# A new order of layer 2 on all engines, its scaled delta kept in PSUM, and slot rows of layer 3 loaded four tiles at a time

## The chip, the cores and the metric

The program runs on 1 core of one Trainium2 chip. The metric is the device time of one execution in microseconds (us), lower is better. Engines are named PE (TensorE matmul), PEld (TensorE weight load), DVE (VectorE), ACT (ScalarE), POOL (GpSimd) and SP (the engine that here only issues DMAs). L2222 is line 2222 of the kernel file before the change.

## The reference

Four layers, each an attention block and a feed-forward block, on x of shape (16, 128, 256), float32, all added to x behind a gate tanh(g). The change touches two of the blocks and nothing that is computed.

```python
# layer 2, attention: 16 heads of 16, keys and values from ctx
q, k, v = proj(x_norm, Wq, bq), proj(ctx, Wk, bk), proj(ctx, Wv, bv)
probs = softmax(clip(q @ k.T / 4, -50, 50))          # masked keys at -50
delta = rs * ((probs @ v) @ Wo.T + bo)
delta = (delta - delta.mean()) / sqrt(delta.var() + 1e-5) * ln_gamma + ln_beta
x = x + tanh(g_xattn[2]) * delta
# layer 2, feed-forward: weights rounded to -1, 0, 1, activations to 8 bits
h = silu(bitlinear(norm(x), w_gate)) * bitlinear(norm(x), w_up)   # 832 wide
x = x + tanh(g_ffn[2]) * bitlinear(h, w_down)
# layer 3, feed-forward: 64 experts of width 96, 6 of them for each token,
# at most 64 tokens per expert and sequence group, and a shared expert of width 192
gx = xp[buf_tok]; g, u = split(gx @ gate_up); eo = (silu(g) * u) @ down * buf_w
x = x + tanh(g_ffn[3]) * (scatter_add(eo) + shared(x))
```

## The kernel before, in words

There is no scheduler. Each layer writes out by hand one program for each engine, and semaphores join them; an engine runs its program strictly in order, so an instruction that waits holds all behind it.

**Layer 2** (`layer_2`). One loop of 19 steps i works on three of the 16 sequences (blocks of 128 tokens) at once: attention of block i, the add of the attention and the start of the feed-forward for y = i - 2, and the end of the feed-forward for f = i - 3. Up to i = 12 each step also produces the keys or the queries of a later pair of blocks ("paired" steps): PE projects (L2127 keys, L2144 queries), ACT adds the bias and rounds to bf16 (`act_bias`, `act_hi`), POOL takes the rest (`pool_rest`, L2603), ACT rounds it (`act_mid`), POOL takes what is left (`pool_lo`, L2607), SP stores the three parts to DRAM and loads them back as stacks for the scores. Even steps also norm a coming pair (`dve_norm_stats`, `pool_norm`).

The work of one step, by name. PE: `pe_scores` twice (half the heads each), `pe_turn_x` in odd steps, `pe_turn_hq` (L2228), `pe_weigh` twice (L2186, probabilities by values, all into one PSUM bank, `av_bank`), `pe_down` (L2235), `pe_values` (L2157), `pe_turn_xq` (L2211), `pe_up` (L2222, gate half and then up half, eight matmuls), `pe_project_out` (L2195, L2197, also into `av_bank`). DVE: `dve_ffn_gate` (L2404 to L2417: the gating, a maximum and the rounding of h), `dve_add_attention` (L2369 scales the delta from PSUM into SBUF, L2373 adds it to x), `dve_ffn_stats`, `dve_clip` twice (L2339), `dve_ffn_quantise` (L2385 to L2394), `dve_normalise` twice (L2347 to L2356), `dve_ffn_add` (L2422), and `dve_delta_stats` (L2361 to L2365) last in the step. ACT: `act_exp` twice, the steps of the production, `act_less_mean`, `act_keep_hq`, `act_values`, `act_keep_xq`, `act_tanh` (L2533). POOL: `pool_delta_root` (L2612, the power -1/2 that L2373 waits for) first in the step, then rest and lo.

In PE's order of before, `pe_project_out(i - 1)` stands last in step i, right behind `pe_up`; the second `pe_weigh` of a block waits until L2369 has read the bank.

**Layer 3, experts** (`l3_experts`). 32 tiles, each two experts by 64 slots. Before them and after them the shared expert runs over 8 blocks. A tile: PE turns its rows (L3366), multiplies by gate and up weights (L3377), turns the hidden part (L3385), multiplies by the down weights (L3392); DVE finds in the rows the tile's own weights and targets (`dve_own`, L3496 to L3502) and gates; ACT scales into `ye_t` (L3569); POOL scatters that to DRAM (L3614). Stages of four tiles are in work at once. SP, one queue, first issues weights of tiles 0 to 9 (576 KB a tile), waits until the slot rows are complete in DRAM, issues the rows of tiles 0 to 5 (140 KB a tile), weights 10 to 19, and then in turn rows n + 6 and weights n + 20 as buffers come free. `dve_own(n)` also waits for the scatter of tile n - 6 (`y_out`), since its target list lies in one of six buffers; `act_store(n)` has the same wait for its `ye_t`.

## Time and profile before

| | |
|---|---|
| median of 3 runs | 2377.92 us (2376.22 to 2381.36) |
| the profiled execution | 2375.99 us, of which 2374.7 us are the span from first to last instruction |
| busy share of the span | PE 83%, DVE 65%, ACT 38%, POOL 23% |
| mean granted PE clock | 0.904 of full speed |
| loop of layer 2 | about 1297 to 1610 us |
| tiles of the experts of layer 3 | about 2237 to 2326 us |

A row of the timeline is one instruction or several of one line merged: start, length, engine, line, operation, count, and in brackets the idle time of the engine before it with what ended that. A row of the waits sums idle time by the pair of waiting line and releasing line. PEclk is the clock granted to TensorE, as a share of its full speed (1.00 is 2.4 GHz, 0.50 is 1.2 GHz); a mixed value is a stretch with both. A DMA share of 1 means that all 16 DMA engines were busy.

### The profile page before, as it was taken

Reading aid. Unit: us, or ns where it says so; the run is one execution under the profiler, and the core shown is the slowest. Engines: PE = TensorE matmul, PEld = TensorE weight load, DVE = VectorE, ACT = ScalarE, POOL = GpSimd, SP = SyncE. Lnnn points to the kernel's source line nnn. Section 1 sums busy time; section 2 is a strip of 40 time slices with the busy share of each in tenths; the row PEclk is TensorE's granted clock in tenths of the full one; section 3 lists DMA queues with packets and bytes.
Section 4 is the critical chain, followed back from the end, with each engine's and each line's share of the span. In section 5 each row is a group of like instructions: output and inputs, shape, how many; then the busy total and the mean of one; then the engine's idle time right before and its main releaser. Section 6 shows DMA issues by size and latency. Waiting matters only on the chain.

```text
span 2374.7 us, 35012 instructions
## 1 busy us (share of the span) xinstructions
PE 1970.2 (83%) x12412; PEld 1270.1 (53%) x12412; DVE 1547.9 (65%) x3614; ACT 907.0 (38%) x2073; POOL 552.8 (23%) x671
## 2 busy tenths in 40 slices
PE   6888889999994878888696677666799999987697
PEld 2444446555553767766523444434467666666344
DVE  7888844444438999999713877762456666655457
ACT  2666631111112655666413444321344443433242
POOL 2212110000002333332303444211013332333231
PEclk7999999999996998999798887767899999998879
DMA  4442220000003333332201452208000000000966
GB/s 97 137 120 61 52 77 14 1 0 1 0 1 81 72 79 73 71 77 59 69 0 47 125 121 64 54 1 274 20 1 30 30 17 4 1 1 1 252 208 266
DMA packets 160348, 157.89 MB, mean 66 GB/s; under 512 B 84504, under 2 KB 139040, under 8 KB 156240
## 3 DMA queue, kind: packets, MB, share of 16 engines
q1 hardware_dynamic: 150864, 146.18, 23.1%
q0 software_dynamic: 6144, 8.82, 1.1%
q8 instruction: 100, 1.64, 0.3%
q10 hardware_dynamic: 3168, 0.66, 0.1%
q14 instruction: 72, 0.59, 0.1%
HBM read 103.14 MB, written 60.82 MB: 69 GB/s over the span
## 4 chain that ended last, share of the span: by engine, by line
PE 56%; DVE 28%; issue 7%; ACT 5%; DMA 2%; POOL 1%; SPq 0%; ACTq 0%; DVEq 0%; POOLq 0%
PE psum L984 10%; PE psum L1004 5%; PE psum L2886 4%; PE psum L2812 3%; PE psum L382 3%; DVE sbuf L535 2%; PE psum L1892 2%; DVE sbuf L1540 2%; PE psum L2879 2%; DVE sbuf L1547 2%; PE psum L2861 2%; PE psum L345 2%; PE psum L2222 1%; PE psum L2848 1%; PE psum L2235 1%
## 5 line engine op out<-in xcount | busy, mean ns | idle before, releaser
L984 PE MATMUL psum<-sbuf 128*128 128x512 f32 (+1 forms) x544 | 245.7, 594 | 0.0
L182 POOL TENSOR_TENSOR sbuf<-sbuf 128x1 f32<-128x1 f32 x128 | 78.0, 612 | 716.8 <-DVE sbuf L174 716.3
L535 DVE TENSOR_REDUCE sbuf<-psum 128x2 f32<-128x512 f32 x256 | 164.8, 684 | 32.4 <-PE psum L345 31.3
L3199 ACT ACTIVATE sbuf<-psum,sbuf 128x128 f32<-128x128 f32 x256 | 113.7, 454 | 188.3 <-DVE sbuf L3034 188.3
L1678 ACT ACTIVATE sbuf<-psum 128x512 f32<-128x512 f32 x256 | 139.8, 597 | 107.6 <-PE psum L1404 93.3
L1110 DVE SCALAR_TENSOR_TENSOR sbuf<-sbuf,psum 128x512 f32<-128x512 f32 (+1 forms) x68 | 46.8, 688 | 196.9 <-ACT sbuf L1173 196.9
L1173 ACT ACTIVATE sbuf<-psum 128x512 f32<-128x512 f32 (+1 forms) x68 | 40.6, 597 | 309.1 <-PE psum L984 309.1
L984 PEld LDWEIGHTS psum<-sbuf 128*128 128x128 f32 (+1 forms) x544 | 100.0, 187 | 105.6 <-issue 103.1
L682 ACT ACTIVATE sbuf<-psum 128x1024 f32<-128x1024 f32 x128 | 130.6, 1022 | 40.9 <-PE psum L367 33.9
L1004 PE MATMUL psum<-sbuf 128*128 128x256 f32 (+1 forms) x544 | 129.2, 380 | 0.7 <-DVE sbuf L1115 0.7
L2812 PE MATMUL psum<-sbuf 128*128 128x256 f32 x512 | 121.8, 393 | 3.4 <-DVE sbuf L2992 1.9
L345 PE MATMUL psum<-sbuf 112*128 112x256 bf16 x512 | 104.4, 289 | 23.1 <-DVE sbuf L535 17.4
L2886 PE MATMUL psum<-sbuf 128*128 128x256 f32 x512 | 121.4, 386 | 1.8 <-DVE sbuf L3048 1.8
L1004 PEld LDWEIGHTS psum<-sbuf 128*128 128x128 f32 (+1 forms) x544 | 102.5, 189 | 37.7 <-issue 24.0
L3271 POOL DMA_INDIRECT l_slot_inputs<-sbuf x96 | 95.4, 993 | 100.9 <-DVE sbuf L3105 67.6
L2812 PEld LDWEIGHTS psum<-sbuf 128*128 128x128 f32 x512 | 99.8, 198 | 25.3 <-issue 6.7
L2879 PE MATMUL psum<-sbuf 128*128 128x512 f32 x128 | 73.1, 654 | 43.5 <-ACT sbuf L3207 43.5
L2886 PEld LDWEIGHTS psum<-sbuf 128*128 128x128 f32 x512 | 95.8, 195 | 13.3 <-DVE sbuf L3048 1.9
L2992 DVE COPY sbuf<-psum 128x1024 f32<-128x1024 f32 x32 | 39.2, 1225 | 89.8 <-ACT sbuf L3170 89.6
L345 PEld LDWEIGHTS psum<-sbuf 112*128 112x128 bf16 x512 | 41.2, 100 | 102.1 <-DVE sbuf L535 64.1
L1547 DVE TENSOR_REDUCE sbuf<-psum 128x8 f32<-128x1024 f32 x64 | 78.0, 1219 | 14.1 <-PE psum L1395 14.1
L1429 PE MATMUL psum<-sbuf 128*16 128x128 f32 x2048 | 74.2, 289 | 13.7 <-DVE sbuf L1569 10.9
(395 smaller groups left out, 4475.5 us busy)
## 6 DMA issues: line engine op xcount, KB each, us to landing
l_pair_outputs<-sbuf SPq DMA_DIRECT2D x24, 512.0 KB, 7.1
sbuf<-in_l_gu_pairs SPq DMA_DIRECT2D x32, 384.0 KB, 7.4
sbuf<-l_pair_outputs SPq DMA_DIRECT2D x16, 768.0 KB, 15.5
sbuf<-l_q_parts SPq DMA_DIRECT2D x16, 384.0 KB
l_q_parts<-sbuf SPq DMA_DIRECT2D x64, 96.0 KB, 2.0
sbuf<-l_q_parts SPq DMA_DIRECT2D x32, 192.0 KB
l_k_parts<-sbuf SPq DMA_DIRECT2D x64, 96.0 KB, 2.0
sbuf<-l_k_parts SPq DMA_DIRECT2D x32, 192.0 KB
```

Source lines behind the costliest of these rows:

```text
L345: last = pe.matmul(score_bank[v % 2][:, j * T0:(j + 1) * T0], q3[0:STACK + 48, h, c * P:(c + 1) * P], k3[0:STACK + 48, h // 4, :], start=T ...
L535: dve.tensor_reduce(top3[:, 2 * hp:2 * hp + 2, c], score_bank[v % 2].rearrange("p (j t) -> p j t", j=2), AXX, ALU.max, negate=True).then_i ...
L682: act.activation(e_t[u % 12], shift_bank[u % 2], ACT.Exp).then_inc(*exped.up())
L984: last = pe.matmul(up_bank[v % 2][0:M, n * BANK:(n + 1) * BANK], wn[:, k, fs], xt_t[blk % 2][:, k, :], start=(k == 0), stop=(k == KD - 1))
L1004: last = pe.matmul(acc[:, i * D:(i + 1) * D], h_t[v % 3][0:M, i * P:(i + 1) * P], w.proj[0:M, f, :], start=(f == 0 and i % 2 == 0), stop=( ...
L1547: dve.tensor_reduce(top_t[b % 2][:, 8 * s:8 * s + 8], split_cols(adapter_bank, 8), AXX, ALU.max, negate=True).then_inc(*a_maxed.up())
L1678: act.activation(e_t[i % 4][:, h * BANK:(h + 1) * BANK], turn_bank[:, h * BANK:(h + 1) * BANK], ACT.Exp).then_inc(*exped.up())
L2812: last = pe.matmul(q_bank[:, j * N:(j + 1) * N], w.wq[:, k, (4 * g + j) * P:(4 * g + j + 1) * P], xt_t[pair % 2][:, k, :], start=(k == 0), ...
L2879: pe.matmul(av_bank, v_t[b % 3][:, g * P:(g + 1) * P], eT_t[u % 2], start=True, stop=True).then_inc(*valued.up())
L2886: last = pe.matmul(out_bank[:, 0:D], o_t[b % 2][:, h * P:(h + 1) * P], w.wo[:, h, :], start=(h == 0), stop=(h == H3 - 1))
L3199: last = act.activation(e_t[u % 3][:, j * P:(j + 1) * P], score_bank[:, j * P:(j + 1) * P], ACT.Exp, bias=mt[:, j:j + 1], scale=rq[:, lo + ...
L3271: pool.indirect_dma_start(out=route.x_slots[:, :], out_offset=bass.IndirectOffsetOnAxis(ap=route.slot[b][:, k:k + 1], axis=0), in_=xr_t[b ...
```

## The change

In layer 2 every engine's program gets another order. On PE the output projection of block y = i - 2 opens step i instead of closing step i - 1, the values come before the first `pe_weigh`, `pe_turn_xq` behind the second, and the first half of the scores of the next block is taken ahead of `pe_up`. On DVE `dve_delta_stats` moves from the end of the step to behind the gate. On ACT the first exp of the next block is done ahead of the tanh, and `act_keep_hq` and `act_values` come before `act_less_mean`. On POOL the root goes behind rest and lo. The scaled delta stays in PSUM: L2369 writes it in place over `av_bank`, L2373 reads it there, and the second `pe_weigh` therefore waits for L2373 (`x_mid`) instead of L2369. `pe_up` signals its gate half and its up half apart; the tanh waits for the first alone. There are four value buffers instead of three.

In layer 3 the rows are loaded four tiles to a DMA, 16 tiles' worth ahead of weights 10 to 19 (tiles 0 to 15 instead of 0 to 5), the later groups from the weight loop: tiles 16 to 19 ahead of weight 23, 20 to 23 ahead of weight 27, 24 to 27 ahead of weight 31, 28 to 31 last of all. `own_t` and `pair_t` exist once for each tile, and `dve_own` no longer waits for a scatter.

```diff
-    v_t = [mem.f32(H2 * 32) for _ in range(3)]
+    v_t = [mem.f32(H2 * 32) for _ in range(4)]
...
         elif b:
-            pe.wait_ge(*y_read.at(b))
+            pe.wait_ge(*x_mid.at(b))
...
-        last.then_inc(*upped.up())
+            last.then_inc(*upped.up())
...
     pe_program:
+        pe_scores(0)
         for i in range(NB + 3):
-            f, y = i - 3, i - 2
-            if i < NB:
-                pe_scores(2 * i)
-            if made_in(i) < 2 * NPAIR:
-                if i % 2 == 0:
-                    pe_queries(i // 2 + 1)
-                else:
-                    pe_keys(i // 2 + 2)
+            f, y, paired = i - 3, i - 2, made_in(i) < 2 * NPAIR
+            if 0 <= y < NB:
+                pe_project_out(y)
+            if paired and i % 2 == 0:
+                pe_queries(i // 2 + 1)
+            if paired and i % 2 == 1:
+                pe_keys(i // 2 + 2)
             if i < NB:
                 pe_scores(2 * i + 1)
...
             if f >= 0:
                 pe_turn_hq(f)
+            if i + 2 < NB:
+                pe_values(i + 2)
             if 1 <= i <= NB:
                 pe_weigh(2 * i - 1)
             if f >= 0:
                 pe_down(f)
-            if i + 2 < NB:
-                pe_values(i + 2)
-            if 0 <= y < NB:
-                pe_turn_xq(y)
             if i < NB:
                 pe_weigh(2 * i)
             if 0 <= y < NB:
+                pe_turn_xq(y)
+            if i + 1 < NB:
+                pe_scores(2 * i + 2)
+            if 0 <= y < NB:
                 pe_up(y)
-            if 1 <= i <= NB:
-                pe_project_out(i - 1)
...
-        d, s = y_t[b % 2][:, 0:D], y_t[b % 2][:, D:D + 16]
-        dve.scalar_tensor_tensor(d, av_bank[:, 0:D], s[:, 6:7], w.gamma, ALU.subtract, ALU.mult).then_inc(*y_read.up())
+        d, s = av_bank[:, 0:D], y_t[b % 2]
+        dve.scalar_tensor_tensor(d, d, s[:, 6:7], w.gamma, ALU.subtract, ALU.mult).then_inc(*y_scaled.up())
...
     dve_program:
             if f >= 0:
                 dve_ffn_gate(f)
             if 0 <= y < NB:
+                dve_delta_stats(y)
+            if i < NB:
+                dve_clip(2 * i)
+            if 0 <= y < NB:
                 dve_add_attention(y)
                 dve_ffn_stats(y)
-            if i < NB:
-                dve_clip(2 * i)
+            if 1 <= i <= NB:
+                dve_normalise(2 * i - 1)
+            if 0 <= y < NB:
+                dve_ffn_quantise(y)
             if i % 2 == 0 and i // 2 + 2 < NPAIR:
                 dve_norm_stats(i // 2 + 2)
-            if 0 <= y < NB:
-                dve_ffn_quantise(y)
-            if 1 <= i <= NB:
-                dve_normalise(2 * i - 1)
             if f >= 0:
                 dve_ffn_add(f)
...
-            if 1 <= i <= NB:
-                dve_delta_stats(i - 1)
...
     act_program:
+        act_exp(0)
...
-            if 0 <= y < NB:
-                act_less_mean(y)
             if f >= 0:
                 act_keep_hq(f)
             if i + 2 < NB:
                 act_values(i + 2)
             if 0 <= y < NB:
+                act_less_mean(y)
                 act_keep_xq(y)
+            if i + 1 < NB:
+                act_exp(2 * i + 2)
+            if 0 <= y < NB:
                 act_tanh(y)
...
     pool_program:
-            if 0 <= y < NB:
-                pool_delta_root(y)
             if j < 2 * NPAIR:
                 pool_rest(j)
                 pool_lo(j)
+            if 0 <= y < NB:
+                pool_delta_root(y)
...
     layer 3:
-        dve.wait_ge(*x_in[n % 6].at(16 * (n // 6 + 1)))
-        if n >= 6:
-            dve.wait_ge(*y_out[n % 6].at(16 * (n // 6)))
+        dve.wait_ge(*x_in[n // 4 % 4].at(16 * (n // 16 + 1)))
...
+    def sp_load_rows(g):
+        if g >= 4:
+            sp.wait_ge(*turned.at(4 * (g - 4) + 4))
+            sp.wait_ge(*own_ready.at(4 * (g - 4) + 4))
+        dst = xe_all[g % 4].rearrange("p (t n) -> p t n", t=4)
+        sp.dma_start(dst, route.x_slots[4 * g * P:4 * (g + 1) * P].rearrange("(t p) n -> p t n", t=4)).then_inc(*x_in[g % 4].up(16))
...
-        for n in range(6):
-            sp_load_rows(n)
+        for g in range(4):
+            sp_load_rows(g)
         for n in range(10, NW3):
             sp_load_weights(n)
-        for n in range(NP):
-            if n + 6 < NP:
-                sp_load_rows(n + 6)
-            if n + NW3 < NP:
-                sp_load_weights(n + NW3)
+        for n in range(NP - NW3):
+            if n in (3, 7, 11):
+                sp_load_rows(n // 4 + 4)
+            sp_load_weights(n + NW3)
+        sp_load_rows(7)
```

## Rows read from the trace of the kernel before

**Rows 1.** Timeline of VectorE, layer 2: start us, us, engine, line, operation
```profile
1392.02 1.02 DVE L2404 SCALAR_TENSOR_TENSOR sbuf<-sbuf,psum 128x832 f32<-128x832 f32 x1
...
1499.52 1.02 DVE L2404 SCALAR_TENSOR_TENSOR sbuf<-sbuf,psum 128x832 f32<-128x832 f32 x1
...
1600.65 1.02 DVE L2404 SCALAR_TENSOR_TENSOR sbuf<-sbuf,psum 128x832 f32<-128x832 f32 x1 [4.58 <-ACT sbuf L2533]
```

**Rows 2.** Waits of VectorE from 1392 to 1500: us in total, times, longest
```profile
DVE sbuf L2361 <- PE psum L2197: 11.5, 6, 2.3
...
DVE sbuf L2347 <- PE psum L2186: 8.0, 6, 2.3
```

**Rows 3.** Timeline of all engines in one loop step of layer 2
```profile
1435.38 0.42 DVE L170 BATCH_NORM_STATS2 sbuf<-sbuf 128x6 f32<-128x256 f32 x1
...
1436.86 0.41 DVE L2385 TENSOR_REDUCE sbuf<-sbuf 128x1 f32<-128x256 f32 x1
...
1438.34 0.44 DVE L2347 STREAM_TRANSPOSE sbuf<-psum 128x256 f32<-128x256 f32 x1
...
1439.61 0.44 DVE L2422 SCALAR_TENSOR_TENSOR sbuf<-psum,sbuf 128x256 f32<-128x256 f32 x1
...
1439.98 0.68 DVE L2339 TENSOR_SCALAR sbuf<-sbuf 128x1024 f32<-128x1024 f32 x1
...
1440.97 1.58 PE L2222 MATMUL psum<-sbuf 128*128 128x416 bf16 x8
...
1442.48 0.69 PE L2195 MATMUL psum<-sbuf 1*128 1x256 f32 x2
...
1444.27 0.43 DVE L2361 BATCH_NORM_STATS2 sbuf<-psum 128x6 f32<-128x256 f32 x1 [1.93 <-PE psum L2197]
...
1444.52 1.95 PE L2127 MATMUL psum<-sbuf 128*128 128x256 f32 x8
...
1445.05 1.02 DVE L2404 SCALAR_TENSOR_TENSOR sbuf<-sbuf,psum 128x832 f32<-128x832 f32 x1
...
1449.61 0.47 DVE L2369 SCALAR_TENSOR_TENSOR sbuf<-psum,sbuf 128x256 f32<-128x256 f32 x1
...
1450.18 1.15 POOL L2607 TENSOR_TENSOR sbuf<-sbuf 128x512 bf16<-128x512 f32 x1 [0.94 <-ACT sbuf L2503]
```

**Rows 4.** Groups by line and shape, 1319 to 1611: count, busy us, mean ns
```profile
L2373 DVE SCALAR_TENSOR_TENSOR sbuf<-sbuf 128x256 f32<-128x256 f32 x16 | 16.5, 1033 | 2.3 <-POOL sbuf L2612 0.3
...
L2612 POOL TENSOR_TENSOR sbuf<-sbuf 128x1 f32<-128x1 f32 x16 | 8.9, 553 | 92.6 <-DVE sbuf L2365 92.6
```

**Rows 5.** Timeline of TensorE before the loop of layer 2
```profile
1272.17 3.78 PE L2144 MATMUL psum<-sbuf 128*128 128x256 f32 x8 [0.69 <-ACT sbuf L2493]
```

**Rows 6.** Windows in layer 3: busy us of each engine, PEclk, DMA share, GB/s
```profile
2230.00:2246.00 16.00, 15.17 (x92) 7.89 (x90) 9.95 (x45) 5.69 (x21) 1.58 (x2) 1.00 1.01 283
...
2246.00:2254.00 8.00, 0.18 (x3) 0.09 (x2) 0.45 (x3) 0.47 (x1) 1.33 (x2) 0.67 1.05 306
...
2254.00:2286.00 32.00, 32.00 (x137) 13.81 (x137) 12.62 (x67) 9.69 (x27) 7.77 (x8) 0.50 0.91 266
...
2286.00:2320.00 34.00, 33.39 (x253) 16.77 (x251) 21.61 (x111) 16.77 (x51) 15.63 (x17) 0.99 0.45 142
```

**Rows 7.** The chain that ended last, in order of time: start, us, what
```profile
2238.82 15.05 DMA sbuf<-l_slot_inputs
```

**Rows 8.** Line 3366, the turning matmuls of the expert loop
```profile
L3366 PE MATMUL psum<-sbuf x64: 272/328/477, 2237.1 to 2318.7; 128*128 128x128 f32 x64
```

**Rows 9.** DMA issues from 2190 to 2345: KB each, median us to landing
```profile
sbuf<-in_l_gu_pairs SPq DMA_DIRECT2D x32, 384.0 KB, 7.4
...
sbuf<-l_slot_inputs SPq DMA_DIRECT2D x32, 140.0 KB
```

**Rows 10.** Waits of VectorE from 2254 to 2330
```profile
DVE sbuf L3496 <- DMA l_pair_outputs<-sbuf: 4.5, 5, 1.9
```

**Rows 11.** Line 3614, the scatters of finished tiles
```profile
DMA to landing us min/median/max: 2.4/2.8/7.2
```

More of the change, by code:

```diff
@@ L2072, in layer_2 @@
     stack = {n: [mem.bf16(H2 * S) for _ in range(2)] for n in "kq"}
-    v_t = [mem.f32(H2 * 32) for _ in range(3)]
+    v_t = [mem.f32(H2 * 32) for _ in range(4)]
     attn_t = [mem.f32(2 * P) for _ in range(2)]
-    y_t = [mem.f32(D + 16) for _ in range(2)]
+    y_t = [mem.f32(16) for _ in range(2)]
     ones, minus_round, row = mem.f32(P), mem.f32(1), mem.f32(D, 1)
@@ L2358, in dve_delta_stats @@
     def dve_delta_stats(b):
-        s, chain = y_t[b % 2][:, D:D + 16], m.chain
+        s, chain = y_t[b % 2], m.chain
         dve.wait_ge(*projected.at(b + 1))
@@ L2609, in pool_delta_root @@
     def pool_delta_root(b):
[L2610 removed]
+        s = y_t[b % 2][:, 8:9]
         pool.wait_ge(*y_var.at(b + 1))
@@ L3332, in l3_experts @@
     sh_t = [mem.f32(SI3) for _ in range(2)]
-    xe_t = [mem.f32(DX) for _ in range(6)]
     xeT_t = [mem.f32(D) for _ in range(2)]
@@ L3337, in l3_experts @@
     ye_t = [mem.f32(D) for _ in range(6)]
-    eq_t, prod_t, own_t = mem.f32(K3), split_cols(mem.f32(2 * K3), 2), [mem.f32(2) for _ in range(6)]
-    pair_t = [mem.f32(1).bitcast(U32) for _ in range(6)]
+    xe_all = [mem.f32(4 * DX) for _ in range(4)]
+    xe_t = [a[:, i * DX:(i + 1) * DX] for a in xe_all for i in range(4)]
+    eq_t, prod_t, own_t = mem.f32(K3), split_cols(mem.f32(2 * K3), 2), [mem.f32(2) for _ in range(NP)]
+    pair_t = [mem.f32(1).bitcast(U32) for _ in range(NP)]
     late = Arena(m.sbuf, B_AT, m.l3_attention_end)
@@ L3344, in l3_experts @@
     w_in = [m.mark(f"expert_weights_loaded_{i}") for i in range(NW3 // 2)]
-    x_in = [m.mark(f"rows_loaded_{i}") for i in range(6)]
+    x_in = [m.mark(f"rows_loaded_{i}") for i in range(4)]
     y_out = [m.mark(f"pairs_scattered_{i}") for i in range(6)]
@@ L3501, in dve_own @@
         dve.wait_ge(*m.chain.now())
-        dve.tensor_scalar(pair_t[n % 6], own[:, 1:2], float(NTOP3), None, ALU.add).then_inc(*own_ready.up())
+        dve.tensor_scalar(pair_t[n], own[:, 1:2], float(NTOP3), None, ALU.add).then_inc(*own_ready.up())
     def dve_combine(b):
```

37 lines of the change are left out of this document (15 added, 22 removed).

## The prediction

> **What bounds the kernel now.** I first read the page: PE is busy for 83% of the span, DVE for 65%, but these are averages over eight blocks of which the change touches two, some 400 of 2375 us. So I read the two stages one at a time, each with the timeline, the waits, and windows.
>
> In layer 2 the thing to see is the step length. `dve_ffn_gate` opens each step, so its first instruction is the step's clock: between the 4th and the 10th of its 16 runs lie six steps of 17.92 us, between the 10th and the last six of 16.86 us [rows 1]. Inside a step DVE stands idle 3.3 us: 11.5 us in six steps for the output projection (L2361) and 8.0 us for the weighing (L2347) [rows 2]. PE in turn waits for the rounded h and for its copy. Neither engine is full; they hand one chain back and forth. Hence order matters, and less work doesn't help unless it lies on that chain.
>
> In layer 3 there are 32 tiles. The turning of the last starts at 2318.7, that of the first at 2237.1 [rows 8]. Three stretches follow each other [rows 6]. Up to 2246 the clock is 1.00, with DMA full at 283 GB/s. From 2246 to 2254 nothing runs: tile 6's rows, issued at 2238.82 behind ten tiles of weights, land 15.05 us later [rows 7]. From 2254 to 2286 the clock is 0.50, and 137 matmuls (15 a tile) are 9 tiles, 3.5 us each; after that, 253 matmuls in 34 us are 2.0 us a tile. The stall costs 7.8 us itself and 9 x 1.5 = 14 us by the slow clock behind it.
>
> **Layer 2, step by step.** I lay measured pieces end to end in the new order, from one start of `pe_up` to the next, in a paired step. The pieces are start-to-start distances in rows 3, so hand-offs are in them.
> - `pe_up` to `pe_project_out`: 1440.97 to 1442.48, 1.5 us. Projection: its reader L2361 starts 1.8 us behind it, at 1444.27, and keys or queries, with no scores between them any more, can follow a little sooner: 1.6.
> - Keys or queries, bias, hi, rest, mid, lo: 1444.52 to the end of L2607 at 1451.33, 6.8 us. The root now stands behind this on POOL: 0.55 [rows 4].
> - L2373, which now reads PSUM, taken at 0.48 (below), the statistics 0.83 (two of them take 1.48, 1435.38 to 1436.86, and an unshared one a little more than half), hand-offs 0.15. Sum so far 11.9 us.
> - The weighing waits for x_mid and delivers 0.3 us after the statistics are done; one normalise is 1.27 (1438.34 to 1439.61), the quantise 1.48 (1436.86 to 1438.34): 14.95.
> - Even steps: two norm statistics 1.48 and the add 0.37 (1439.61 to 1439.98), then `pe_up`: 16.85. Odd steps: turn, copy and hand-offs, 1.0: 15.95.
>
> The mean is 16.4. PE's clock will be low in some of the short matmuls behind a wait, as it is now; I add 0.25: 16.65, against 17.92, a saving of 1.3 us. This holds for steps 3 to 12 at least, nine of them up to the 10th gate: 9 x 1.3 = 11.5 us. So the DVE wait for the projection goes, but what is late next is the root: DVE has finished gate, delta statistics and clip (4.56 + 0.78 + 0.60) some 2 us before `pool_lo` and the root are through, and waits for POOL where it never did.
>
> In the unpaired steps that cover is gone and DVE's own list decides: gate 4.56 (1445.05 to 1449.61), delta statistics 0.78 (1444.27 to 1445.05), two clips 1.2, the two delta instructions 1.0, statistics 0.83, two normalises 2.54, quantise 1.48, add 0.37: 12.8. With 1.6 us of waits for root, weighing and tanh it is 14.4. The last six steps are one paired and five of these: (16.65 + 5 x 14.4) / 6 = 14.8 against 16.86, 6 x 2.06 = 12.4 us. Layer 2 saves 11.5 + 12.4, say 24 us.
>
> Edits inside that sum. The tanh starts after the gate half of `pe_up`: 4 of 8 matmuls earlier, 0.75 us, but the exp now ahead of it on ACT eats about as much; it is in the 1.6. The delta in PSUM: L2373 takes 1.03 us on average with both inputs in SBUF [rows 4], L2422, the same operation and shape with one input in PSUM, 0.44 [rows 3]. I take 0.48; bounds 0.44 and 1.03, that is 0 to 0.6 us a step, so up to 9 us less gain. Writing PSUM from DVE appears in no row; nearest is L2369's 0.47 into SBUF, taken unchanged, up to 1.0 as the far bound (8 us). The extra memset of a value buffer, 0.5 us, lies before the wait of DVE for the weight sums, on no path. The second weighing waits for L2373 instead of L2369, 0.5 us later plus the root; behind it on PE are down, the first weighing and turn_xq, counted. Stacks: scores of the next block are taken a few us earlier in a step, while their DMAs are issued a whole step before; cover some 9 us.
>
> L2422 shows no price for a PSUM source. The Trainium skill (VectorE: DVE Perf Modes, the TRN2 errata) gives VectorE 120 fixed cycles for a PSUM source and 58 for SBUF, which speaks against this edit; by it, an estimate, L2373 would be 0.065 us dearer, 1.0 us over 16 steps. By the row it is nothing.
>
> **Layer 3, step by step.** Tiles 6 to 15 are there early, so the stall at tile 6 goes (7.8 us), and with it the fall of the clock (14 us): 21.8 us on paper. But DMA is full from 2230 on, and bytes do not go away. A tile's weights are 384 KB [rows 9] and 192 KB, its rows 140 KB. SP is one queue and the rows of tiles 20 to 23 are issued behind rows 0 to 19 and weights 10 to 26: 24 x 0.143 + 17 x 0.590 = 13.5 MB, plus 16 scatters of 0.13 MB, 15.6 MB in all. At 283 GB/s [rows 6] from 2226 that is 55 us, 2281. At 2.0 us a tile PE wants them at 2237 + 40 = 2277: a stall of 4 us. Then 0.57 MB of rows, four weights and scatters, 3.4 MB, 12 us: tiles 24 to 27 at 2293. The idle stretch at 2246 took the clock from 1.00 to 0.50 within it (0.67 mean over 8 us, [rows 6]), so I take it that 4 us do that too. Then tiles 20 to 28 go at 3.5 us as nine tiles did, the clock comes back at about 2313, and the last turn is at 2313 + 2 = 2315, against 2318.7: a gain of 4 us. Bounds: the clock never comes back, 2281 + 11 x 3.5 = 2319.5, nothing gained; the clock holds, tile 24 at 2293, the last at 2307, 12 us; DMA at 306 GB/s [rows 6], 16 us.
>
> The stall falls between dense stretches. The Trainium skill (TensorE: Matmul & The Clock Gate, HAM oscillation) tells of a loop in which each wait for DMA returns the array to its low clock; by that rule layer 3 gains the 4 us and not the 12.
>
> `dve_own`'s waits for scatters, 4.5 us in five times [rows 10], go. `act_store` keeps such a wait, but six tiles, 12 us, after the scatter it waits for; landings take at most 7.2 [rows 11]. SP's later loads wait for tiles long turned.
>
> **The sum.** -24 - 4 = -28 us on the profiled execution's 2375.99: 2348. The median of the runs shown lies 1.9 us above the profiled one, so 2350.
>
> **The rivals.**
> - *The clock holds.* The new order spreads PE's waits into more and shorter ones (I lay 1.1, 2.4 and 1.5 us in a paired step), and layer 2 keeps 1.00 through the matmuls behind them. At half the clock eight matmuls of the same size take 3.78 us [rows 5] instead of 1.9, so these run twice as fast; with 2 us of them slow in four steps of ten, an estimate, that is 0.8 us a step, 12 us in 15 steps. In layer 3 the stall is below what costs the clock: 12 instead of 4. 2350 - 20 = 2330. For it: the gap that cost the clock in layer 3 was 8 us long. Against: more pieces of work stand behind a wait.
> - *Half lost to the root.* Keys and queries stand on the chain now. At the low clock they take 3.78 us [rows 5], not 1.95 [rows 3], and the projection, in the same ratio less its fixed part, 2.9, not 1.6: 3.2 us a step. If that hits half of the ten paired steps, 16 us are gone, and 2 of layer 3: 2368. Against it: keys and projection run right behind `pe_up` at the high clock now [rows 3], and the new order keeps this neighbour.
> - *Slower.* The same place, all ten steps: 32 us lost in layer 2, 8 us above before, and layer 3 gains nothing: 2386. The mechanism decides from 28 / 3.2 = 9 of the ten steps on. For it only that the chain leaves no cover; the rest as above.
> - *Nothing.* The saved waits return elsewhere to the last microsecond: within 0.2%, which is 4.8 us and about what a measurement of this kernel can tell from no change.
>
> **How the numbers follow.** The forecast (its own range 2340 to 2360) has 0.45, the clock holds 0.28, half lost 0.15, slower 0.09, nothing 0.03. The range 2326 to 2372 takes in the first three and leaves out 0.15 or so. Faster 0.87, same 0.04, slower 0.09.
>
> **What would show it.** Layer 2: gate to gate 16 to 17.5 us, alternating, and 14 to 15 after the last paired step; L2373 near 0.5 us, and a new wait of DVE for POOL's root of about 2 us in paired steps, none in the others; the DVE wait for the projection near zero. A wait below 1 us there, or a step above 17.5, proves the chain wrong. Layer 3: no gap at 2246 less the shift; rows of tiles 20 or 24 awaited 3 to 5 us; the clock in the 30 us behind. If that gap is missing, the DMA sum is wrong, and the time falls to the low end. If L2361 or the weighing still waits 2 us a step, PE's list is longer than I laid it, and the gain halves.

## The result, and the profile after

The changed kernel takes 2354.89 us (median of four, 2344.89 to 2359.69) beside 2379.64 us for the kernel before: a ratio of 0.9886 (95% interval 0.9844 to 0.9929), 25 us faster on medians. The profiled execution is the fastest of the four, 2344.89 us with a span of 2343.5 us, and so 10 us below the median; the sums of this section are made on the spans of the two profiled executions, which differ by 31.2 us. Line numbers of the changed kernel are up to three higher: L2422, L2612, L3052 and L3366 of before are now L2423, L2614, L3054 and L3369.

**Layer 2.** The timeline of the changed kernel at the same three runs of the gate as [rows 1], the 4th, the 10th and the last:

```profile
1389.12 1.02 DVE L2404 SCALAR_TENSOR_TENSOR sbuf<-sbuf,psum 128x832 f32<-128x832 f32 x1 [0.80 <-ACT sbuf L2534]
...
1492.35 1.02 DVE L2404 SCALAR_TENSOR_TENSOR sbuf<-sbuf,psum 128x832 f32<-128x832 f32 x1 [0.80 <-ACT sbuf L2534]
...
1581.20 1.02 DVE L2404 SCALAR_TENSOR_TENSOR sbuf<-sbuf,psum 128x832 f32<-128x832 f32 x1 [3.49 <-ACT sbuf L2534]
```

From the 4th to the 10th are 103.2 us, 17.2 a step (17.92 before), from the 10th to the last 88.9 us, 14.8 a step (16.86). The last add of layer 2 comes at 1590.80, 19.4 us earlier than before. The waits of VectorE between 1392 and 1500, which answer to [rows 2]:

```profile
DVE sbuf L2373 <- POOL sbuf L2614: 15.7, 6, 5.1
...
DVE sbuf L2404 <- ACT sbuf L2534: 4.8, 6, 1.0
...
DVE sbuf L2347 <- PE psum L2186: 0.4, 1, 0.4
```

The waits for the projection are gone and the one for the weighing has shrunk to 0.4 us. In their place stand a wait for the root, 2.6 us a step, and one for the tanh, 0.8 us a step. The groups by line and shape answer to [rows 4]:

```profile
L2369 DVE SCALAR_TENSOR_TENSOR psum<-psum,sbuf 128x256 f32<-128x256 f32 x16 | 7.7, 484 | 0.0
...
L2373 DVE SCALAR_TENSOR_TENSOR sbuf<-psum,sbuf 128x256 f32<-128x256 f32 x16 | 7.7, 483 | 27.5 <-POOL sbuf L2614 27.1
```

The write of the delta into PSUM takes 0.484 us, and L2373, which reads it there, 0.483 us, as against 1.033 on average before.

**Layer 3, experts.** Windows over the stage (busy us of PE, PEld, DVE, ACT and POOL, then PEclk, DMA share, GB/s), which answer to [rows 6]:

```profile
2219.00:2235.00 16.00, 15.17 (x87) 8.18 (x87) 9.17 (x42) 5.65 (x21) 0.97 (x1) 1.00 1.06 334
...
2235.00:2251.00 16.00, 16.00 (x122) 8.09 (x122) 10.71 (x57) 8.02 (x26) 7.79 (x8) 1.00 1.04 336
...
2251.00:2267.00 16.00, 16.00 (x122) 8.07 (x121) 10.72 (x57) 8.02 (x26) 7.79 (x8) 1.00 1.05 334
...
2267.00:2275.00 8.00, 6.59 (x53) 3.31 (x49) 4.64 (x24) 3.39 (x11) 3.80 (x4) 1.00 1.06 328
```

The line of the turning matmuls answers to [rows 8]:

```profile
L3369 PE MATMUL psum<-sbuf x64: 272/273/332, 2227.5 to 2288.0; 128*128 128x128 f32 x64
```

The first turn is at 2227.5, the last at 2288.0: 60.5 us, where it was 81.6. There is no idle stretch at tile 6, the clock stays at 1.00, and at a full DMA share 328 to 336 GB/s are moved, where [rows 6] had 283 to 306. Only at the turn of tile 24, near 2273, is there a gap, of 1.4 us. The trace puts it down to VectorE's L3469, for which this turn doesn't wait; the tile's rows were issued at 2259.09, and their late arrival is my reading, not shown.

**The account** of the 31.2 us: layer 2 gives 19.4, the experts 21.1, what follows them 0.5. Between layer 2 and the experts, where nothing was changed, 9.8 us are lost. The line that adds the attention of layer 3, once for each of 16 blocks, shows most of it; in the kernel before (first row), in the changed one (second), and in the experiment with rows asked for sooner (third), whose code is the same up to there:

```profile
L3052 DVE SCALAR_TENSOR_TENSOR sbuf<-psum,sbuf x16: 476/478/480, 1740.9 to 2197.6; 128x256 f32<-128x256 f32 x16
```

```profile
L3054 DVE SCALAR_TENSOR_TENSOR sbuf<-psum,sbuf x16: 476/477/482, 1721.5 to 2187.4; 128x256 f32<-128x256 f32 x16
```

```profile
L3054 DVE SCALAR_TENSOR_TENSOR sbuf<-psum,sbuf x16: 476/477/479, 1722.3 to 2177.7; 128x256 f32<-128x256 f32 x16
```

First to last: 456.7, 465.9 and 455.4 us. The same code took anything from 455 to 466 us in the profiles of this study, and the changed kernel itself took 457.2 in a second one. So these 9 us are no price of the change that every execution pays; they lie in the spread of single executions.

### The profile page after: what moved, and what is told of

It is laid out like the page before. It is cut to its first block, busy times and chain, and to the rows that moved or that the text cites. A ratio compares the mean times of both kernels' runs of the same rounds, so it can differ in the third digit from the quotient of the medians.

```text
span 2343.5 us, 34927 instructions
## 1 busy us (share of the span) xinstructions
PE 1949.3 (83%) x12382; PEld 1261.0 (54%) x12412; DVE 1538.9 (66%) x3616; ACT 905.9 (39%) x2073; POOL 553.2 (24%) x671
## 4 chain that ended last, share of the span: by engine, by line
PE 56%; DVE 27%; issue 7%; ACT 5%; POOL 2%; DMA 1%; SPq 0%; ACTq 0%; another core or an unknown queue 0%; DVEq 0%; POOLq 0%
PE psum L984 10%; PE psum L1004 5%; PE psum L2888 4%; PE psum L2814 4%; PE psum L382 3%; DVE sbuf L535 3%; PE psum L1892 2%; DVE sbuf L1540 2%; PE psum L2881 2%; PE psum L2863 2%; DVE sbuf L1547 2%; PE psum L345 2%; PE psum L2850 1%; PE psum L2222 1%; PE psum L367 1%
## 5 line engine op out<-in xcount | busy, mean ns | idle before, releaser
L345 PE MATMUL psum<-sbuf 112*128 112x256 bf16 x512 | 105.1, 290 | 21.9 <-DVE sbuf L535 17.3
```

The source lines that it names most:

```text
L345: last = pe.matmul(score_bank[v % 2][:, j * T0:(j + 1) * T0], q3[0:STACK + 48, h, c * P:(c + 1) * P], k3[0:STACK + 48, h // 4, :], start=T ...
```

## The experiments

All were run beside the kernel before on the same chip; a ratio is to that. There are four such sets, in which the kernel before took 2379.64 us (changed), 2377.54 (the two parts and the two places of the root), 2367.90 (the next four rows) and 2371.27 (the last four), so medians are compared within a set and ratios across. Of each kernel the table shows the median, and from its profile the two step lengths of layer 2 (4th to 10th gate, 10th to last) and the expert stage (first to last turn).

| kernel | median us | ratio (95% interval) | steps us | experts us |
|---|---|---|---|---|
| before | | | 17.9, 16.9 | 81.6 |
| changed | 2354.89 | 0.9886 (0.9844 to 0.9929) | 17.2, 14.8 | 60.5 |
| layer 2 part alone | 2363.71 | 0.9939 (0.9918 to 0.9960) | 17.0, 14.6 | 84.2 |
| layer 3 part alone | 2366.36 | 0.9946 (0.9924 to 0.9967) | 18.2, 16.3 | 65.9 |
| root between | 2334.57 | 0.9812 (0.9783 to 0.9840) | 15.5, 14.4 | 60.2 |
| root first | 2324.90 | 0.9786 (0.9757 to 0.9815) | 15.3, 14.5 | 60.1 |
| rows one by one | 2354.84 | 0.9921 (0.9891 to 0.9951) | 17.3, 14.9 | 79.7 |
| two groups late | 2341.71 | 0.9884 (0.9853 to 0.9914) | 17.3, 14.8 | 67.7 |
| delta in SBUF | 2342.39 | 0.9886 (0.9860 to 0.9913) | 17.1, 14.3 | 65.9 |
| one signal | 2350.35 | 0.9923 (0.9898 to 0.9948) | 17.1, 15.3 | 78.9 |
| changed, again | 2338.36 | 0.9853 (0.9832 to 0.9874) | 17.1, 14.4 | 78.3 |
| rows sooner | 2333.29 | 0.9832 (0.9812 to 0.9851) | 16.9, 15.0 | 59.1 |
| root first, rows sooner | 2315.55 | 0.9761 (0.9743 to 0.9779) | 15.3, 14.5 | 59.1 |
| the same, delta in SBUF | 2310.62 | 0.9742 (0.9723 to 0.9761) | 15.3, 14.2 | 59.1 |

The layer 2 of the changed kernel stands unedited in six rows (changed, layer 2 part alone, one by one, two late, again, sooner): its steps are 16.9 to 17.3 and 14.4 to 15.0 us. That is the noise against which a step is read. The layer 3 of the changed kernel stands unedited in seven rows, and its stage is anything from 60.1 to 78.9 us; the section on the slot rows comes back to that. A ratio therefore can't tell 5 us of layer 2 from the luck of layer 3.

### The two parts alone

The layer 2 part alone has layer 3 as before; the layer 3 part alone has layer 2 as before.

> The layer 2 part alone; layer 3's slot rows are loaded as in the kernel before. The theory (the two parts are independent): layer 2 keeps its new step times (f3 to f9 17.2 us a step, f9 to f15 14.8), its last x_done comes 19 us earlier, and the expert stage is the old one with its stall near tile 6 and the low clock behind it; about 19 us (15 to 20) faster than before, 0.992 of it. Rival 1 (layer 2's order costs the attention of layer 3 some 10 us through its clock, which is where the trace of the changed kernel lost them): about 10 us faster, and layer 3's block times drift against those of before as they did in the changed kernel. Rival 2 (that loss was the variation of one execution): no such drift here.

> The layer 3 part alone; layer 2 as in the kernel before. The theory (the stall at tile 6 was late rows, and its removal also keeps the clock): the expert stage runs 20 us shorter, with the granted clock at 1.00 throughout and no wait above 2 us; 18 to 21 us faster than before. Rival (the prediction's reading: the DMA rate of 283 GB/s sets the stage, and the changed kernel's 335 GB/s was luck of that execution): a stall of 4 us near tile 20 and a low clock behind it, 4 us faster. A third: the two parts do not add up, since their sum of 39 us is more than the 25 us by which the medians differ; then one of them gives less than its stage showed.

They give 13.8 and 11.2 us on medians, together 25.0, as much as the whole change: the parts add up, within intervals of some 5 us each. Neither hit its number. In the profile of the layer 2 part layer 2 is 21 us shorter, but the expert stage of before, stall and all, takes 84.2 us, not 81.6, and layer 3's attention 463 us; the drift is therefore there without being tied to a part (the layer 3 part alone shows 462). In the layer 3 part the stage shrank by 15.7 us, and it has waits for rows after all, 1.4 us at tile 20 and 2.6 at tile 24, as its waits of TensorE show (L3367 is its turning line):

```profile
PE psum L3367 <- DMA sbuf<-l_slot_inputs: 4.0, 2, 2.6
```

### The place of the root

```diff
             if j < 2 * NPAIR:
                 pool_rest(j)
-                pool_lo(j)
             if 0 <= y < NB:
                 pool_delta_root(y)
+            if j < 2 * NPAIR:
+                pool_lo(j)
```

That is the root between the two subtractions; in the other kernel it stands ahead of both, as before the change.

> The changed kernel with GpSimd's root of the variance put between its subtractions 'rest' and 'lo' of the paired steps, not behind both. The theory (the root comes late because two subtractions stand ahead of it): VectorE's wait for the root falls from 2.6 us a paired step to about 1.2, TensorE's wait for the scores' clip by the same, and ten paired steps are 1 us shorter each: 7 to 12 us faster than the changed kernel. Rival (the second subtraction then comes later, the 'lo' rows for the keys' turn are late, and TensorE waits there instead): the wait for the root falls and the step stays at 17.2 us.

> The changed kernel with GpSimd's root ahead of both subtractions, the place it had in the kernel before. The theory: VectorE's wait for the root falls to some 0.6 us, but GpSimd now stands at the root until VectorE has the variance, with both subtractions queued behind it; the gain is at most that of the root between them, 0 to 10 us faster than the changed kernel. Rival (the subtractions are on no path that matters): 2 us a paired step, 20 us faster. Other rival (they are, and their lateness costs more than the root's): slower than the changed kernel by 5 us or more.

The root first is faster than forecast: 0.9786, beside 0.9886 and (measured again) 0.9853 for the changed kernel, is 16 to 24 us. The root between gains 10 to 18 us by the same two ratios, and 7 to 12 were forecast. The paired step falls from 17.2 to 15.5 and 15.3 us, more than the 1 us forecast for the root between. The gates of the kernel with the root first:

```profile
1382.26 1.02 DVE L2404 SCALAR_TENSOR_TENSOR sbuf<-sbuf,psum 128x832 f32<-128x832 f32 x1 [0.81 <-ACT sbuf L2534]
...
1474.12 1.02 DVE L2404 SCALAR_TENSOR_TENSOR sbuf<-sbuf,psum 128x832 f32<-128x832 f32 x1 [1.75 <-ACT sbuf L2534]
...
1561.11 1.02 DVE L2404 SCALAR_TENSOR_TENSOR sbuf<-sbuf,psum 128x832 f32<-128x832 f32 x1 [3.49 <-ACT sbuf L2534]
```

Its waits from 1392 to 1500, of VectorE, of GpSimd and of TensorE, and under them those of VectorE with the root between:

```profile
DVE sbuf L2404 <- ACT sbuf L2534: 6.1, 7, 1.8
...
DVE sbuf L2347 <- PE psum L2186: 1.9, 3, 0.9
```

```profile
POOL sbuf L2614 <- DVE sbuf L2365: 42.3, 7, 8.4
```

```profile
PE psum L2235 <- ACT sbuf L2542: 7.6, 6, 1.5
...
PE psum L2186 <- DVE sbuf L2373: 1.8, 3, 0.6
```

```profile
DVE sbuf L2404 <- ACT sbuf L2534: 5.4, 7, 1.3
...
DVE sbuf L2373 <- POOL sbuf L2614: 5.1, 3, 2.8
```

With the root first no wait for it is left. GpSimd stands 42.3 us at the root until the variance is there, with both subtractions queued behind it. That lateness is not free: ScalarE, which rounds what the first subtraction leaves, comes later to the copy of h (L2542), and TensorE now waits 7.6 us for that. But its wait for L2373 before the weighing fell from 12.3 us in six times to 1.8 in three, and the balance is 1.9 us a step (1.6 in the pair of the last set, 16.9 to 15.3). So the rival was nearly right: the lateness of the subtractions costs less than that of the root, whose 0.55 us of work had been waiting behind 2.3 us of them. The root between keeps a third of the waits (5.1 us in three steps). The clean price is that of the last set, on one chip, rows sooner against rows sooner with the root first: 2333.29 (2329.88 to 2334.80) to 2315.55 (2314.87 to 2317.05), 17.7 us, and in their profiles 19 us from the first gate to the last add.

### The delta in PSUM

```diff
-        d, s = av_bank[:, 0:D], y_t[b % 2]
+        d, s = y_t[b % 2][:, 0:D], y_t[b % 2][:, D:D + 16]
-            pe.wait_ge(*x_mid.at(b))
+            pe.wait_ge(*y_scaled.at(b))
```

> The changed kernel with the scaled delta put back into SBUF, so that TensorE's weigh waits for the scaling alone and not for the addition to x behind the root. In the changed kernel TensorE waits for that addition 2.05 us a paired step. Theory (the PSUM delta ties TensorE to the root): that wait goes, values and weigh run 2.6 us sooner in a paired step, but VectorE still waits for the root itself, so the step shortens by 0.5 to 1.5 us only: 5 to 15 us faster than the changed kernel. Rival (VectorE is the bound of the step, its wait for the root stays, and the write to SBUF costs as much as that to PSUM): within 0.2% of the changed kernel.

> As the one beside it, and the scaled delta in SBUF, so that TensorE's weigh waits only for the scaling. With the delta in SBUF alone the last six steps of layer 2 took 14.25 us against 14.8, and the paired ones 17.07 against 17.2. Theory (with the root early, TensorE's wait for the addition to x is 0.3 us a step, and the PSUM delta still holds the bank through it): 0.3 to 0.5 us less in each of 16 steps, 4 to 8 us faster than the kernel beside it. Rival (with the root first the addition follows at once, and the bank comes free as soon either way): the same within 0.2%.

On the changed kernel it is the rival's case as far as can be told: its ratio of 0.9886 is that of the changed kernel (0.9886, and 0.9853 when run again), and the paired step is within the noise; its last six steps, 14.25 us, lie 0.15 under the lowest of the six rows. With the root first it is 4.9 us faster (2309.05 to 2313.44 against 2314.87 to 2317.05), but not by the mechanism expected: the first gate comes 1.6 us earlier in the profile, where nothing differs, and the last add of layer 2 only 0.3 us, so that layer 2 itself is no shorter; 4.2 us arise between that add and the first block of layer 3, where the granted clock is 0.73 and not 0.65 in the first 22 us. Why it is, stays open; that the clock there depends on how layer 2 ends is my guess.

The price of L2373 is clear, and it hangs on GpSimd as much as on the source that the prediction reasoned from. Its line in four kernels: before (SBUF), delta in SBUF on the changed kernel, root first (PSUM), and root first with the delta in SBUF:

```profile
L2373 DVE SCALAR_TENSOR_TENSOR sbuf<-sbuf x16: 483/1201/1409, 1324.4 to 1590.7; 128x256 f32<-128x256 f32 x16
```

```profile
L2373 DVE SCALAR_TENSOR_TENSOR sbuf<-sbuf x16: 483/485/485, 1331.9 to 1572.6; 128x256 f32<-128x256 f32 x16
```

```profile
L2373 DVE SCALAR_TENSOR_TENSOR sbuf<-psum,sbuf x16: 483/483/484, 1328.7 to 1553.6; 128x256 f32<-128x256 f32 x16
```

```profile
L2373 DVE SCALAR_TENSOR_TENSOR sbuf<-sbuf x16: 483/1284/1298, 1324.5 to 1550.8; 128x256 f32<-128x256 f32 x16
```

With both inputs in SBUF it takes 0.485 us when GpSimd waits beside it and a median of 1.28 when GpSimd subtracts; with one input in PSUM 0.483 in either case. The timelines of the last kernel and of the one with the root first show the neighbour, a subtraction of 1.15 us:

```profile
1448.71 1.15 POOL L2605 TENSOR_TENSOR sbuf<-sbuf 128x512 f32<-128x512 f32 x1
...
1448.86 1.28 DVE L2373 SCALAR_TENSOR_TENSOR sbuf<-sbuf 128x256 f32<-128x256 f32 x1
```

```profile
1449.52 1.15 POOL L2605 TENSOR_TENSOR sbuf<-sbuf 128x512 f32<-128x512 f32 x1
...
1449.68 0.48 DVE L2373 SCALAR_TENSOR_TENSOR sbuf<-psum,sbuf 128x256 f32<-128x256 f32 x1
```

The Trainium skill (GPSIMD Engine Reference, Specifications) says that VectorE and GpSimd share their SBUF interfaces and that a VectorE instruction with two SBUF inputs contends; these rows agree. The estimate of 65 ns more for a PSUM source, which the prediction worked out from the Trainium skill (VectorE: DVE Perf Modes, the TRN2 errata), is not borne out: 483 ns with one input in PSUM stand beside 485 with both in SBUF.

### One signal for both halves of the matmul

```diff
-        act.wait_ge(*upped.at(2 * f + 1))
+        act.wait_ge(*upped.at(2 * f + 2))
```

> The changed kernel, but the tanh waits for both halves of pe_up, as before, and not for the gate's half alone. Theory: the tanh starts one half of pe_up later (0.7 to 0.9 us of matmuls), and VectorE already waits 0.8 us a step for the tanh, so each of the sixteen steps is 0.5 to 0.9 us longer: 8 to 14 us slower than the changed kernel. Rival (VectorE comes to the gate later than that because of its wait for the root, and in the paired steps nothing changes): 2 to 5 us slower, from the last six steps alone.

The paired steps are as long as before (17.1 us), but not as they were. From 1392 to 1500 VectorE waits 8.0 us in six times for the tanh instead of 4.8, and for the root, 15.7 us in the changed kernel, not at all. The time went into VectorE's own instructions. L2418, the last instruction of `dve_ffn_gate`, in the changed kernel (first) and in this one:

```profile
L2418 DVE TENSOR_SCALAR sbuf<-sbuf x16: 653/654/655, 1341.3 to 1585.2; 128x832 f32<-128x832 f32 x16
```

```profile
L2418 DVE TENSOR_SCALAR sbuf<-sbuf x16: 653/1127/1607, 1342.3 to 1587.9; 128x832 f32<-128x832 f32 x16
```

In each of the six paired steps it takes 1.60 us and starts together with the first subtraction, and the clips (L2339) take 1.06 us on average instead of 0.76; one of the two runs beside the second subtraction. So the wait for the root was slack of VectorE, and the later start and the slower instructions used it up. The last six steps take 15.3 us, 0.3 above the noise. That is the rival's size, 2 to 5 us. The whole kernel is at 0.9923, but its profile also has a long expert stage, so that the ratio doesn't price the signal.

### The slot rows

Rows one by one: the same order and buffers, but a DMA for each tile.

```diff
-        sp.dma_start(dst, route.x_slots[4 * g * P:4 * (g + 1) * P].rearrange("(t p) n -> p t n", t=4)).then_inc(*x_in[g % 4].up(16))
+        for n in range(4 * g, 4 * g + 4):
+            sp.dma_start(xe_t[n % 16], route.x_slots[n * P:(n + 1) * P]).then_inc(*x_in[g % 4].up(16))
```

Two groups late: tiles 8 to 15 are asked for behind weights 10 to 19.

```diff
-        for g in range(4):
+        for g in range(2):
             sp_load_rows(g)
         for n in range(10, NW3):
             sp_load_weights(n)
+        for g in range(2, 4):
+            sp_load_rows(g)
```

> The changed kernel with the slot rows in the same order and the same 16 tiles of buffer, but loaded by one DMA for each tile of 140 KB, not one for four tiles of 560 KB. It separates the two things that the layer 3 part does. Theory A (the rows come in time because they are asked for ahead of the weights of tiles 10 to 19, and the form of the DMA is nothing): no stall in the expert loop, the granted clock stays at 1.00, last turn 60 us after the first, the same time as the changed kernel within 0.2%. Theory B (the DMA of four tiles is what raises the rate from the 280 GB/s of before to the 335 GB/s of after at the same full share): 280 to 300 GB/s in the first 24 us of the loop, so rows or weights come late near tile 16 to 20, a stall of 3 us or more there, a lower clock behind it, and 8 to 20 us slower than the changed kernel.

> The changed kernel with groups 2 and 3 of the slot rows (tiles 8 to 15) asked for behind the weights of tiles 10 to 19, and groups 0 and 1 ahead of them. Theory (what counts is what stands ahead of the rows in the queue): the weights of ten tiles are 5.9 MB, 17.6 us at 335 GB/s, and come behind 1.15 MB of rows; the rows of tile 8 land about 22 us behind the loop's start of loading and tile 8 is turned 16 us after the first; a stall of 5 to 9 us at tile 8, the granted clock falls to 0.50 behind it, and the stage takes 75 to 82 us, not 60.5; 13 to 20 us slower than the changed kernel. Rival (the stall alone, the clock holds): 6 us slower. Rival 2 (at 335 GB/s the rows come in time): no change.

One by one, theory B held for the rate. Its windows, and below them the waits of TensorE for rows:

```profile
2221.00:2237.00 16.00, 15.17 (x108) 7.96 (x108) 10.50 (x53) 6.56 (x21) 3.04 (x4) 1.00 1.00 279
...
2237.00:2253.00 16.00, 16.00 (x122) 8.09 (x124) 10.68 (x56) 8.02 (x25) 7.80 (x9) 1.00 1.04 327
...
2253.00:2258.00 5.00, 0.56 (x4) 0.10 (x4) 0.70 (x3) 0.50 (x2) 1.80 (x2) 0.89 1.06 332
```

```profile
PE psum L3369 <- DMA sbuf<-l_slot_inputs: 7.7, 3, 4.5
```

While the first 16 tiles of rows are under way, 279 GB/s are moved at a share of 1.00; in the next window, with few rows in it, 327. The rows come 7.7 us late in three times, PE is idle near 2255, and the stage takes 79.7 us. In the window at the same place, from 4 us ahead of the first turn, ten of the eleven profiles with DMAs of 560 KB show 315 to 338 GB/s, and one, that of one signal, 294. The Trainium skill (DMA: Bandwidth & Descriptors, Bandwidth) advises to batch DMAs, and its table, of single DMAs issued from GpSimd, has the rate rise with the size; these kernels agree in direction. Two things stay open. SP needed 8.8 us to issue the 16 DMAs where it needs 2.2 for four, and whether that or the size lowers the rate was not tried apart. And the 79.7 us are no price of the form by themselves, since the stage of the unedited kernel can be nearly as long, as the next profile shows. The late groups, however, came in time (theory wrong, rival 2 right for tile 8): only 0.3 us is lost there, and the stage's length of 67.7 us is due to a wait of 2.3 us at tile 24 and the low clock behind it.

That sends one back to the changed kernel, which was run again beside a kernel that asks for its last groups sooner:

```diff
-            if n in (3, 7, 11):
-                sp_load_rows(n // 4 + 4)
+            if n in (1, 5, 8, 10):
+                sp_load_rows({1: 4, 5: 5, 8: 6, 10: 7}[n])
             sp_load_weights(n + NW3)
-        sp_load_rows(7)
```

> The changed kernel itself, unedited, as the base for the three kernels beside it and to see whether its expert stage of 60.5 us is its usual one. Theory (the layer 3 part has little to spare: a group of rows lands late by a few us in some executions, near tile 16 or 24, and the clock falls behind it): the median is 0.988 to 0.991 of before, and this profile shows an expert stage from 60 to 80 us with waits for slot rows in it. Rival (the stage is always 60.5 us, and the executions differ elsewhere): 60 to 61 us here too.

> The changed kernel with the last four groups of slot rows asked for sooner among the weights: ahead of the weights of tiles 21, 25, 28 and 30, not of 23, 27, 31 and after the last. The buffers that they need are turned by then, so no wait is added. Theory (the late groups stand behind 1.7 MB of weights that are wanted later than they are): no wait for slot rows, the granted clock stays at 1.00, the expert stage takes 60 us, and the median is 4 to 12 us below the changed kernel's on the same chip, with less spread. Rival (the DMA engines are full until the last rows land, so that the total of bytes sets the wait and not its order): a wait of 2 to 5 us stays, now for weights, and the time is the same within 0.2%.

The unedited kernel in this second profile, by three windows, the waits of TensorE, and the chain that ended last (start, us, what):

```profile
2205.00:2221.00 16.00, 15.17 (x91) 8.12 (x89) 9.56 (x43) 5.66 (x20) 0.97 (x1) 1.00 1.06 338
...
2237.00:2253.00 16.00, 12.87 (x97) 6.36 (x95) 8.72 (x45) 6.72 (x20) 7.77 (x8) 0.97 1.05 323
...
2257.00:2283.00 26.00, 26.00 (x113) 11.40 (x113) 9.78 (x52) 8.62 (x23) 6.81 (x7) 0.50 0.43 127
```

```profile
PE psum L3369 <- DMA sbuf<-l_slot_inputs: 3.7, 1, 3.7
```

```profile
2236.72 16.77 DMA sbuf<-l_slot_inputs
```

The rows of tiles 20 to 23, issued at 2236.72, land 16.77 us later; PE waits 3.7 us, the clock falls to 0.50 for the next ten tiles, and the stage takes 78.3 us, 18 more than in the first profile of the very same program. With the rows sooner that group is issued at 2232.53, 15.4 us behind the first turn and not 23.8, and nothing waits for a slot row. Its issues on SP, windows, and turning line:

```profile
2232.53 1.57 SPq L3635 DMA_DIRECT2D sbuf<-l_slot_inputs  x1
```

```profile
2209.00:2225.00 16.00, 15.17 (x90) 8.31 (x90) 9.41 (x42) 5.65 (x20) 0.97 (x1) 1.00 1.06 344
...
2225.00:2241.00 16.00, 16.00 (x125) 8.07 (x122) 10.70 (x57) 7.98 (x24) 7.78 (x8) 1.00 1.05 334
...
2241.00:2257.00 16.00, 16.00 (x126) 8.07 (x120) 10.71 (x57) 7.97 (x24) 7.77 (x8) 1.00 1.05 344
...
2257.00:2263.00 6.00, 6.00 (x49) 3.02 (x45) 4.13 (x22) 2.99 (x9) 2.74 (x3) 1.00 1.07 324
```

```profile
L3369 PE MATMUL psum<-sbuf x64: 272/273/329, 2217.1 to 2276.2; 128*128 128x128 f32 x64
```

The DMA share is as full and the rate as high: order, not bytes.

Seven profiles of this study have the unedited layer 3. Of each the table shows how long before the first turn SP issues the first rows, the waits for rows at their tiles (with the gap at tile 24 that the trace of the changed kernel and that of the root first name otherwise), how long the clock is at 0.50 from there on, and the stage, all in us.

| kernel | first rows ahead | waits | low clock | experts |
|---|---|---|---|---|
| root first | 13.7 | 0.6 at tile 24 | none | 60.1 |
| root between | 13.5 | 1.1 at 24 | none | 60.2 |
| changed | 13.2 | 1.4 at 24 | none | 60.5 |
| delta in SBUF | 12.6 | 0.6 at 20, 3.1 at 24 | 7 | 65.9 |
| changed, again | 11.3 | 3.7 at 20 | 37 | 78.3 |
| one signal | 11.1 | 2.1 at 16 | 41 | 78.9 |
| layer 3 part alone | 11.0 | 1.4 at 20, 2.6 at 24 | 7 | 65.9 |

Where the rows are issued 13.2 us ahead or more, the stage is 60 us; where less, there is a wait with the low clock behind it. SP may issue them only when the slot rows are complete in DRAM, for which it waits 13.4 us in the changed kernel and 15.8 in its second profile. That is an order seen in seven profiles and was not set by an experiment. With the rows sooner the stage is 59.1 us in all three profiles, at 13.0, 12.2 and 11.8 us ahead.

The five runs with the rows sooner lie between 2329.88 and 2334.80, those of the unedited kernel between 2333.13 and 2348.56. The medians differ by 5.1 us, which the intervals don't separate; the upper half of the range is not seen again in five runs.

> The root of the variance ahead of both subtractions on GpSimd and the slot rows asked for sooner, both in one kernel. Theory (two stages, nothing shared): layer 2 as with the root first alone (15.3 us a paired step, last x_done at 1570 us), the expert stage 60 us, 2315 to 2325 us on a chip where the kernel before takes 2372, that is 0.976 to 0.980 of it. Rival (the shorter stage 2 is paid for by later clock falls in layer 3): no better than 0.981.

As the theory had it: 0.9761, five runs within 2.2 us of each other, 23 us (1.0%) under the changed kernel on that chip. With the delta in SBUF as well it is 0.9742, the fastest of all.

## Why the prediction was right, and where it was not

The forecast of 2350 us (faster) stands beside 2354.89, inside its own range. The sums of its two stages were off, in opposite directions.

- **The last six steps, 14.8 us.** Measured 14.8. In the five unpaired ones VectorE's own work and hand-offs are 12.0 us a step, not 12.8, and its waits 2.5 (12.3 in five, 8.5 of them for the tanh), not 1.6. The account had the right parts, and the errors of two of them cancel; that is luck.
- **The paired step, 16.65 us against 17.92.** Measured 17.2, and from the loop's start to the 10th gate 7 us were gained, not 11.5; that is nearly all of the difference between 24 and 19.4 us in layer 2. Five of the six steps up to there take 16.6 to 17.0 us, within 0.35 of the laid 16.65, and VectorE waits 2.1 us a step for the root in them (10.6 in five), as forecast. The sixth takes 19.15, with a wait of 5.1. The term mis-sized is therefore the 0.25 us a step laid for PE's low clock: the mean lies 0.56 above 16.65, and 0.42 of that is the sixth step alone. In it the rival *half lost to the root* is to be seen at work: in the timeline of PE, projection and keys of an ordinary step (first two rows) and of that one (last two), and the windows of both places.

```profile
1441.09 1.13 PE L2197 MATMUL psum<-sbuf 128*128 128x256 f32 x4
...
1442.05 1.89 PE L2127 MATMUL psum<-sbuf 128*128 128x256 f32 x8
...
1474.64 2.07 PE L2197 MATMUL psum<-sbuf 128*128 128x256 f32 x4
...
1476.51 2.77 PE L2127 MATMUL psum<-sbuf 128*128 128x256 f32 x8
```

```profile
1440.00:1448.00 8.00, 6.69 (x38) 5.05 (x37) 5.93 (x12) 3.99 (x7) 3.04 (x5) 0.95 0.03 13
...
1473.00:1476.00 3.00, 3.00 (x7) 1.67 (x6) 2.66 (x3) 0.17 (x1) 1.98 (x3) 0.50 0.12 45
```

The clock was 0.50 from 1473 to 1476, and from the start of the projection to the end of the keys are 4.6 us instead of 2.9. The mechanism was right, its share one step in six and not half. Four of the six profiles with this layer 2 have one such step of 19.2 us; in this one the second step of the loop, 18.2 us at a clock of 0.80, is slow too. Steps above 17.5 us were the prediction's sign of a wrong chain; these two are above, and the other seven up to the 10th gate, 16.3 to 17.4 us, speak for the chain. The alternation of even and odd steps that I laid is not there.
- **The root behind the subtractions, "0.55".** It was priced as work on a chain that I took for given. The chain was a choice: moved ahead, it takes 1.6 to 1.9 us out of a paired step. That the new place costs more than it gives was not among the rivals.
- **L2373 at 0.48 us.** The number was right to 5 ns and the reason incomplete: in the changed kernel GpSimd waits beside it, and both inputs in SBUF give the same 0.485. Only with the root first does the PSUM source make the difference, 0.48 instead of 1.28.
- **The tanh's own signal.** Without it the paired steps are as long as with it, since VectorE has slack in them, and the others 0.3 us or a little more as far as these runs can tell; the forecast gave it no number of its own.
- **Layer 3, "at 283 GB/s ... a stall of 4 us".** This is the step that failed for the profiled execution. The rate was read where rows moved in DMAs of 140 KB, and the change makes them 560 KB: 334 GB/s. With it the same sum puts the rows of tiles 20 to 23 at 2226 + 15.6 MB / 334 GB/s = 2273, 36 us behind the first turn. PE wants them at 37 us, not at the laid 40, since the first four tiles take 5 us and not 8; so there is no stall, and the stage gave 21.1 us, not 4. The prediction's sign, that without the gap the DMA sum is wrong, held; the low end of the time that it named with it didn't come, for layer 2 and the spread stood against it. And the sum was close to an edge: in the second profile the group lands 40.6 us behind the first turn (forecast 44), PE waits 3.7 us (forecast 4), the clock falls to 0.50, and the stage takes 78.3 us (forecast 78). Both outcomes belong to this kernel. The table of seven profiles suggests what decides between them, the lead of the first rows over the first turn, which the prediction took as fixed (2226 and 2237); that it is the cause was not shown.
- **The clock after a wait.** "I take it that 4 us do that too" held: the clock fell after the 3.7 us, and after waits of 2.1, 2.6 and 3.1 us in other profiles; after the gap of 1.4 us it stayed at 1.00. How long it stays low was taken from one case, nine tiles. It was 37 us at the wait of 3.7 and 41 at that of 2.1, but 7 at those of 2.6 and 3.1. What decides that stays open. The rule cited for the fall (the Trainium skill, TensorE: Matmul & The Clock Gate, HAM oscillation) fits those four and not the gap of 1.4 us.
- **Own waits and stores.** Neither a wait of `dve_own` nor one of `act_store` for a scatter is on the path after; their removal was not tried by itself, and its share stays open.

So the forecast came out because 17 us too little in layer 3 met 4.6 too much in layer 2 and some 10 us of spread that belongs to neither. That these cancelled is luck; layer 2 alone was forecast on its mechanism.

## What to carry to other kernels

When an order is rewritten, price each short instruction by what it queues behind, not by its own length: half a microsecond of GpSimd work behind two subtractions cost 18 us, 0.8% of this kernel. Don't take a DMA rate of before for transfers whose form the change alters. And where a buffer arrives with a microsecond or two to spare, look at two profiles and at the spread of the runs: a late group that drops TensorE's clock can cost many times its own lateness (18 us for 3.7), and issuing it two or three loads sooner cost nothing here. A wait that goes away is no gain in itself: without the wait for the root VectorE ran slower beside GpSimd, and the step stayed as long.

## What the runs showed of the hardware

- VectorE's scalar_tensor_tensor of 128x256 float32 with both inputs in SBUF takes 0.48 us alone and about 1.28 beside a GpSimd subtraction of 128x512; with one input in PSUM it takes 0.48 beside the same subtraction.
- A tensor_scalar of 128x832 float32 from SBUF to SBUF, with one tensor as input, takes 0.65 us alone and 1.60 beside that subtraction.
- Slot rows (1120 bytes a partition and tile) mixed with weights move at 279 GB/s as DMAs of 140 KB and at 315 to 338 as DMAs of 560 KB in ten profiles of eleven (294 in the other), in the same 16 us of the stage. The DMA share there is 0.99 in the first case and 1.04 or 1.05 in the others.
- A wait of 3.7 us at full clock brought ten tiles at 0.50 behind it, some 15 us more on a stage of 60. At waits of 2.6 and 3.1 us, in two other profiles, it was at 0.50 for 7 us only.
